# Keys' second rotary projection replaced by four ScalarE copies of 32-row blocks, from the fourth pair on

## The chip, the cores and the metric

The kernel runs on one core of a Trainium2 chip. The metric is the device time of the program in microseconds (us), taken as the median of several runs. Engines are named as in the profile: PE is TensorE's matmuls, PEld its weight loads, DVE is VectorE, ACT is ScalarE, POOL is GpSimd, SP is SyncE, which issues the DMAs.

## The reference

One decoder layer with three residual parts, each followed by a layer norm, on x of 32 sequences of 64 rows and 256 features:

```
x = layernorm(x + self_attention(x))            # 16 heads of 16, causal
x = layernorm(x + cross_attention(x, ctx))      # 8 heads of 8, rotary embedding
x = layernorm(x + ffn(x))                       # two quantised products, 256 -> 1024 -> 256
```

In the cross attention the second axis (64) holds the channels and the third (256) the positions. The part that the change touches is the rotary embedding of the keys:

```
k = Wk @ c + bk                                  # 64 x 256
half = k.shape[-1] // 2                          # of the 8 channels of a head
rot = concatenate([-k[half:], k[:half]])         # within each head
k = k * cos(pos) + rot * sin(pos)
```

`rot` is k with the two halves of each head's channels exchanged, and one half negated.

## The kernel before

**Tiling.** The 32 sequences are worked on as 16 pairs (`NPAIR`), each a tile of 128 partitions (two sequences of 64) and 256 columns. A first phase does both attentions of all pairs, and a second one the ffn.

**The first phase** is a software pipeline. `body(i)` is written once for each engine, runs for i = -1 to 15, and has 16 steps s. The body of i does the cross attention's maxima (`max_tile`, L971 on DVE) and exponentials (`exp_tile`, L780 on ACT) of pair i, some work of `prev = i - 1`, `nxt = i + 1`, `j = i + 2`, and the self attention and key projection of `a = i + 3`. In what follows a turn is one such body, and a step is one s. In each step PE does two products for a maximum (L581) and two for an exponential (L609), and in most also a group for something else. The instructions of each engine stand in its queue in the order in which they are written and are done in that order; engines meet in semaphores (`wait`).

**Maxima.** The products of a step land in one of two banks `mx_b`; `max_ready` lets PE write a bank when DVE has reduced the tile of two steps before. The exponentials have two banks `e_b` and `exp_ready` in the same manner.

**The general banks.** Three banks `g_b0`, `g_b1`, `g_b2` of 128 x 512 float32 serve all else. PE's helper `use` (L474) makes every use of a bank wait until the readers of the use before are done:

```
def use(bank, ev, pair, step):
    if bank.name in last_read:
        pe.wait_ge(*last_read[bank.name])
    last_read[bank.name] = (ev.sem, ev.at(pair, step))
```

**The rotary embedding.** `rotary_proj` multiplies the input with two weight matrices: "A", the projection, and "B", the same with its rows exchanged so that it gives the exchanged channels (`swap`). A goes to columns 0 to 255 of the bank, B to 256 to 511 (L558, L559; each float32 matmul is two records in the profile). The rows of both are laid out in the order of `by_parity` and `split`, so that the exchange is one of blocks of 32 partitions: 0 with 1, and 2 with 3. `rotate` on DVE then does two steps (L962): m = 0 is (A + bias) * cos, m = 1 is (B + bias) * sin, each with one count on `ro_sb`. Each is 128 x 256. `split_parts` on POOL adds the two and splits the sum into three bfloat16 parts (L906 to L916), which SP stores and loads again in expanded form (`KA`).

For the keys of a pair with number over 2 (`fresh`), that is pairs 3 to 15 in turns i = 0 to 12, PE does `rotary_proj("k", g_b[2], a)` in step 9, and DVE `rotate("k", g_b[2], a)` in step 10. The earlier three pairs' keys use other banks and are not touched.

**What stands around it.** In the order of the queues:

- PE: step 9 the key projection and `x_out_proj` of prev (L263); step 10 the transpose of the maxima (`max_transpose`, L595) and values (L626); step 11; step 12 `v_proj` (L495, from the pair after), `transpose_p(a)` (L523), values; step 13 `self_pv` (L536). `transpose_p` transposes the self attention's normalised probabilities `SP`, its first group into `g_b2` and its second into `g_b1`:

```
wait(pe, s_norm, a, 1)
for g in range(2):
    ps = use(g_b[2 - g], pt_sb, a, g + 1)
```

- DVE: step 4 the row maxima of the self scores (L924) after PE's `scores` (L510), and a subtraction (L932); step 7 another; step 9 `max_tile`, then `self_sum` (L941, L943); step 10 `max_tile`, `mt_low` (MR, L977), `rotate`, `norm2_stats` of prev (Y, L296, L299, L301); step 11 `max_tile`.
- POOL: `self_norm` (L898) after `self_sum`, `rstd` for prev (L314 to L318), `split_parts("k", a)`.
- ACT: step 9 the exponential and `mt_copy` (L774); steps 10 and 11 the exponentials; step 12 the exponential and `pt_copy` (L759), which copies the transposes. For some pairs a piece of the weights' preparation stands in step 11.

Of the kernel before, what the change touches and what calls it, by code (L numbers as in the profile page):

```python
# [21 lines left out]
ACT = mybir.ActivationFunctionType  # L22
# [5 lines left out]
P = 128  # L28
D = 256
# [51 lines left out]
def build_layer(nc, x, xT, ctx, wpT, woT, xW, xB, rows, w1T, w2T, attn_tables, rotary_tables, out):  # L81
    with ExitStack() as outer:
        es = outer

        def sb(name, shape, dt=F32):
            return es.enter_context(nc.sbuf_tensor(name, shape, dt))
# [4 lines left out]
        def sem(name):  # L91
            return es.enter_context(nc.semaphore(name))

        def event(name, steps=1):
            return Event(sem(name), steps)
# [12 lines left out]
        xw = {n: xw_all[:, k, :] for k, n in enumerate(XW)}  # L108
# [26 lines left out]
        g_b = [bank(f"g_b{n}") for n in range(2)]  # L135
# [26 lines left out]
        rot = {n: sb("rot_" + n, [P, 2, D]) for n in "qk"}  # L162
        full = {n: sb("full_" + n, [P, D]) for n in "qk"}
        part = {n: sb("part_" + n, [P, 3, D], BF16) for n in "qk"}
        QA = sb("QA", [P, 6, HH, D], BF16)
        KA = sb("KA", [P, 6, HH, D], BF16)
        VA = sb("VA", [P, 2, 2, 2, XH, 32])
# [33 lines left out]
        ro_ps = {n: event(n + "_ps") for n in "qk"}  # L201
        ro_sb = {n: event(n + "_rot", 2) for n in "qk"}
        split = {n: event(n + "_split", 5) for n in "qk"}
        xv_ps, xv_sb = event("xv_ps"), event("xv_sb")
        expand = {n: [sem(f"expand_{n}{p}") for p in range(3)] for n in "qk"}
        stored = {n: [sem(f"stored_{n}{p}") for p in range(2)] for n in "qk"}
        parts_hbm = {n: [nc.dram_tensor(f"parts_{n}{p}", (4, P, D), BF16, kind="Internal").ap() for p in range(2)] for n in "qk"}
# [14 lines left out]
        def wait(eng, ev, pair, step):  # L222
            eng.wait_ge(ev.sem, ev.at(pair, step))
# [5 lines left out]
        def real(pair):  # L229
            return 0 <= pair.v < NPAIR  # L230

        def fresh(pair):

            return real(pair) and pair.v > 2
# [236 lines left out]
        def _(pe):  # L471
# [76 lines left out]
            def rotary_proj(n, bank, j):  # L548

                pe.wait_ge(ld_cross, NCROSS)  # L550
                if n == "q":
                    wait(pe, ln1, j, 7)
                    src = XALL[:, j.v, :]
                else:
                    pe.wait_ge(ld_c[j.slot], 16 * (j.laps + 1))
                    src = C[:, j.slot, :]
                ps = use(bank, ro_sb[n], j, 2)
                nc.tensor.matmul(ps[:, 0:D], xw[n + "A"], src, start=True, stop=True)  # L558
                nc.tensor.matmul(ps[:, D:2 * D], xw[n + "B"], src, start=True, stop=True).then_inc(ro_ps[n].sem, 1)  # L559

            def xv_proj(v):

# [164 lines left out]
        def _(act):  # L727
# [40 lines left out]
            def mt_copy(i, b, g):  # L768
                wait(act, mt_ps, i, b + 1)
                before = i.plus(b - 1)  # L770
                if b == 1 or has(i, 1):
                    act.wait_ge(mrow[before.ring][1 - b], NMROW * (before.rounds + 1))

                nc.scalar.activation(MR[0:16, :], g_b[g][0:16, 0:P], ACT.Copy, scale=-1.0).then_inc(mt_sb.sem, 1)  # L774
# [14 lines left out]
            def norm1(a):  # L789
                wait(act, ln1, a, 6)  # L790
                nc.scalar.activation(XALL[:, a.v, :], Y1[:], ACT.Identity, bias=rs1[:, 2:3], scale=rs1[:, 1:2]).then_inc(ln1.sem, 1)

            def xv_copy(v):
                wait(act, xv_ps, v, 1)
                if has(v, 2):
                    wait(act, pv, v.plus(-2), 8)
                act.wait_ge(s_ones, 2)
                nc.scalar.activation(VA[:, v.p].rearrange("p s b h c -> p (s b) h c")[:, :, :, 0:XC],
                                     g_b[1][:, 0:D].rearrange("p (q h c) -> p q h c", q=4, h=XH),
                                     ACT.Copy).then_inc(xv_sb.sem, 1)  # L800
# [40 lines left out]
            def body(i):  # L841
                prev, nxt, j, a = i.plus(-1), i.plus(1), i.plus(2), i.plus(3)
                for s in range(16):
                    if real(i):
                        exp_tile(i, s)
                    if s == int(i.v == NPAIR - 1) and real(prev):
                        u_copy(prev)
                    if s == 0 and real(j):
                        norm1(j)
                    if s == 0 and fresh(a):  # L850
                        qk_copy(a, g_b[2])
                    if s == 1 and real(i):
                        mt_copy(i, 1, 0)
                    if s == 5 and real(prev):
                        at_copy(act, prev, 2)
                    if s == 7 and real(nxt):
                        xv_copy(nxt)
                    if s == 7 and fresh(a):
                        self_exp(a, 1)
                        self_exp(a, 0)  # L860
                    if s == 9 and real(nxt):
                        mt_copy(nxt, 0, 0)
                    if s == 12 and real(a):
                        pt_copy(a)
                    if s == 13 and real(prev):
                        norm2(act, prev)
                    if s == 13 and real(a):
                        ao_copy(a)
                    if s == 15 and real(i.plus(4)):
                        v_copy(i.plus(4), g_b[0])  # L870
                    if s == 15 and real(prev):
                        square_sum(act, prev)
                    if s in (3, 11) and W_SUM <= i.v < W_SUM + 4:
                        weight_sum(2 * (i.v - W_SUM) + s // 8)
                    if s in (3, 11) and W_ROUND <= i.v < W_ROUND + 4:
                        weight_round(2 * (i.v - W_ROUND) + s // 8)
# [43 lines left out]
        def _(dve):  # L920
# [35 lines left out]
            def rotate(n, bank, j):  # L956

                wait(dve, ro_ps[n], j, 1)
                if has(j, 1):
                    wait(dve, split[n], j.plus(-1), 2)  # L960
                for m, tab in ((0, cos), (1, sin)):
                    nc.vector.scalar_tensor_tensor(out=rot[n][:, m, :], in0=bank[:, D * m:D * m + D],  # L962
                                                   scalar=xb[n + "AB"[m]], in1=tab[:],
                                                   op0=ALU.add, op1=ALU.mult).then_inc(ro_sb[n].sem, 1)

# [41 lines left out]
            def body(i):  # L1007
                prev, nxt, j, a = i.plus(-1), i.plus(1), i.plus(2), i.plus(3)
                for s in range(16):
                    ahead, n = tile_at(i, s + AHEAD)  # L1010
                    if real(ahead):
                        max_tile(ahead, n)
                    if s == 2 and real(i):
                        mt_low(i, 1, 0)
                    if s == (2 if i.v >= 0 else 5) and real(j):
                        rotate("q", g_b[1], j)
                    if s == 3 and real(prev):
                        u_norm(dve, prev, 2)
                    if s == 4 and fresh(a):
                        row_max(a, 1)  # L1020
                        row_max(a, 0)
                        minus_max(a, 1)
                    if s == 7 and fresh(a):
                        minus_max(a, 0)
                    if s == 9 and real(a):
                        self_sum(a)
                    if s == 9 and real(a) and not fresh(a):
                        rotate("k", e_b[1], a)
                    if s == 10 and real(nxt):
                        mt_low(nxt, 0, 0)  # L1030
                    if s == 10 and fresh(a):
                        rotate("k", g_b[2], a)
                    if s == 10 and real(prev):
                        norm2_stats(dve, prev, 1)
                    if s == 14 and real(prev):
                        norm2_max(dve, prev)
                    if s == 15 and real(a):
                        norm1_stats(a)
                    if s == 14 and i.v == W_TOTAL:
                        weight_scale()  # L1040
                    if s == 4 and i.v == NPAIR - 1:
                        mean_square(dve, 0)
                    if s == 11 and i.v == NPAIR - 1:
                        factors(dve, 0)
                    if s == 1 and W_ROUND <= i.v - 1 < W_ROUND + 4:
                        for step in range(2):
                            for piece in range(2):
                                weight_clip(2 * (i.v - 1 - W_ROUND) + piece, step)
# [27 lines left out]

            prologue()
            bodies(dve, body)


# [469 lines left out]
```

## Time and profile before

| | |
|---|---|
| median of 3 runs | 543.01 us (540.65, 543.01, 547.83) |
| the profiled execution | 539.41 us, of which the span from the first to the last instruction is 537.3 us |
| busy in the span | PE 428.1 us (80%), DVE 442.1 (82%), ACT 374.3 (70%), POOL 287.1 (53%) |
| mean granted TensorE clock | 0.873 of full speed |

The profile is one execution, and its times are in microseconds from the start of the span. A line such as L559 is that of the kernel before, printed above. The busy time of PE is that of its matmuls, which overlap one another; what one costs the queue is read from start to start. "Idle before" names the engine and line whose work ended the wait.

### The profile page before, as it was taken

Reading aid. Unit: us, or ns where it says so; the run is one execution under the profiler, and the core shown is the slowest. Engines: PE = TensorE matmul, PEld = TensorE weight load, DVE = VectorE, ACT = ScalarE, POOL = GpSimd, SP = SyncE. Lnnn points to the kernel's source line nnn. Section 1 sums busy time; section 2 is a strip of 40 time slices with the busy share of each in tenths; the row PEclk is TensorE's granted clock in tenths of the full one; section 3 lists DMA queues with packets and bytes.
Section 4 is the critical chain, followed back from the end, with each engine's and each line's share of the span. In section 5 each row is a group of like instructions: output and inputs, shape, how many; then the busy total and the mean of one; then the engine's idle time right before and its main releaser. Section 6 shows DMA issues by size and latency. Waiting matters only on the chain. (4 is left out here: it accounts for less than half of the span.)

```text
span 537.3 us, 11851 instructions
## 1 busy us (share of the span) xinstructions
PE 428.1 (80%) x4098; PEld 231.1 (43%) x4098; DVE 442.1 (82%) x948; ACT 374.3 (70%) x700; POOL 287.1 (53%) x390
## 2 busy tenths in 40 slices
PE   6567799999999999999999999998876602555553
PEld 5354445445454554545545555443332201333332
DVE  3755787989889889799998998988749959999993
ACT  2232266678687786777877867677778778999983
POOL 5841646475474655645557446450124547767653
PEclk9676799999999999999999999999998855555557
DMA  6125326442332322323223232221000000000001
GB/s 226 46 77 182 93 57 187 113 114 69 82 96 63 113 70 67 108 52 111 71 64 112 66 95 69 61 89 42 3 0 1 1 0 1 11 30 20 31 30 40
DMA packets 51674, 37.07 MB, mean 69 GB/s; under 512 B 21408, under 2 KB 47648, under 8 KB 51488
## 3 DMA queue, kind: packets, MB, share of 16 engines
q1 hardware_dynamic: 51328, 36.10, 22.9%
q8 instruction: 33, 0.54, 0.4%
q10 hardware_dynamic: 288, 0.23, 0.2%
q14 instruction: 25, 0.20, 0.1%
HBM read 24.52 MB, written 10.49 MB: 65 GB/s over the span
## 5 line engine op out<-in xcount | busy, mean ns | idle before, releaser
L971 DVE TENSOR_REDUCE MX<-mx_b 128x2 f32<-128x512 f32 x256 | 167.1, 679 | 26.5 <-PE mx_b L581 25.4
L780 ACT ACTIVATE PB<-e_b 128x512 f32<-128x512 f32 x256 | 148.1, 592 | 55.2 <-PE e_b L609 54.0
L581 PE MATMUL mx_b<-KA,QA 48*128 48x256 bf16 x512 | 97.6, 275 | 11.5 <-DVE MX L971 10.8
L609 PE MATMUL e_b<-QA,KA 50*128 50x256 bf16 x512 | 97.1, 274 | 1.0 <-DMA QA<-MR 0.7
L626 PE MATMUL u_b<-PB,VA 128*32 128x256 f32 x1024 | 84.0, 391 | 2.0 <-ACT PB L780 1.5
L898 POOL TENSOR_TENSOR SP<-SP,srec 128x1024 f32<-128x1024 f32 x15 | 28.5, 1901 | 79.1 <-DVE srec L943 79.1
L581 PEld LDWEIGHTS mx_b<-KA,QA 48*128 48x128 bf16 x512 | 29.6, 94 | 86.7 <-issue 47.1
L1301 PE MATMUL r_b<-identh,Q 128*128 128x128 f16 x128 | 16.2, 305 | 39.5 <-ACT Q L1214 39.5
L1246 POOL TENSOR_TENSOR H<-H,row_tab 128x1024 f32<-128x1024 f32 x15 | 35.4, 2363 | 21.4 <-ACT H L1204 17.9
L1307 PE MATMUL z_b<-w2q,Q2T 128*128 128x256 bf16 x128 | 28.5, 400 | 19.3 <-ACT Q2T L1225 19.3
L888 POOL TENSOR_TENSOR KM<-QK,att_tab 128x512 f32<-128x512 f32 x31 | 32.0, 1052 | 21.4 <-ACT QK L734 21.4
L486 PE MATMUL g_b<-XT,wp 128*128 128x128 f32 x256 | 34.5, 290 | 4.7 <-DMA wp<-in_wpT 4.7
L626 PEld LDWEIGHTS u_b<-PB,VA 128*32 128x32 f32 x1024 | 22.4, 108 | 30.8 <-ACT PB L780 16.6
L314 POOL TENSOR_TENSOR rs<-mv,epsc 128x1 f32<-128x1 f32 x32 | 6.1, 189 | 54.3 <-DVE mv L301 38.3
L486 PEld LDWEIGHTS g_b<-XT,wp 128*128 128x128 f32 x256 | 31.5, 200 | 7.9 <-DMA wp<-in_wpT 4.7
L1301 PEld LDWEIGHTS r_b<-identh,Q 128*128 128x128 f16 x128 | 12.2, 139 | 46.6 <-ACT Q L1214 46.5
L609 PEld LDWEIGHTS e_b<-QA,KA 50*128 50x128 bf16 x512 | 28.5, 94 | 7.4 <-ACT PB L780 3.2
L759 ACT ACTIVATE PT<-g_b 128x512 f32<-128x512 f32 x32 | 17.7, 595 | 19.2 <-PE g_b L523 18.9
L1307 PEld LDWEIGHTS z_b<-w2q,Q2T 128*128 128x128 bf16 x128 | 15.9, 135 | 28.8 <-ACT Q2T L1225 23.4
L924 DVE TENSOR_REDUCE smax<-g_b 128x8 f32<-128x512 f32 x32 | 20.6, 686 | 8.8 <-PE g_b L510 8.8
L523 PE MATMUL g_b<-att_tab,SP 128*128 128x128 f32 x128 | 18.8, 296 | 8.8 <-POOL SP L898 4.7
L1422 DVE BATCH_NORM_STATS2 sth<-H 128x6 f32<-128x512 f32 x32 | 20.4, 680 | 3.5 <-ACT H L1208 3.5
(172 smaller groups left out, 1017.0 us busy)
## 6 DMA issues: line engine op xcount, KB each, us to landing
KA<-parts_k SPq DMA_DIRECT2D x64, 96.0 KB
QA<-parts_q SPq DMA_DIRECT2D x64, 96.0 KB
parts_q<-part_q SPq DMA_DIRECT2D x32, 128.0 KB, 1.9
parts_k<-part_k SPq DMA_DIRECT2D x16, 192.0 KB, 2.1
C<-in_ctx SPq DMA_DIRECT2D x16, 128.0 KB, 3.1
X<-in_x SPq DMA_DIRECT2D x16, 128.0 KB, 2.9
out_y<-O SPq DMA_DIRECT2D x16, 128.0 KB, 1.7
XT<-in_xT SPq DMA_DIRECT2D x15, 128.0 KB, 2.2
```

The source lines that it names most:

```text
L486: last = nc.tensor.matmul(ps[:, P * c:P * c + P], wp[:, k, P * c:P * c + P], XT[:, a.p, k, :], start=k == 0, stop=k == 1)
L581: m = nc.tensor.matmul(mx_b[n % 2][:, D * k:D * k + D], QA[low:low + K_MAX, 2 * i.ring + b, h, P * u:P * u + P], KA[low:low + K_MAX, 2 * i ...
L609: m = nc.tensor.matmul(e_b[n % 2][:, D * k:D * k + D], KA[low:low + K_EXP, 2 * i.ring + b, h, P * sc:P * sc + P], QA[low:low + K_EXP, 2 * ...
L626: last = nc.tensor.matmul(u_b[32 * j:32 * j + 32, D * b:D * b + D], VA[:, i.p, sc, b].rearrange("p h c -> p (h c)")[:, own:own + 32], PB[: ...
L780: nc.scalar.activation(PB[:, n % 4].rearrange("p e t -> p (e t)"), e_b[n % 2][:, :], ACT.Exp, scale=XC ** -0.5).then_inc(e_sb.sem, 1)
L888: ops.tensor_tensor(KM[:, c], QK[:, 2 + c, :].unsqueeze(1).broadcast_to([P, 4, P]), kmask.unsqueeze(2).broadcast_to([P, 4, P]), ALU.mult). ...
L898: ops.tensor_tensor(SP[:], SP[:], srec[:].unsqueeze(2).broadcast_to([P, SH, SEQ]), ALU.mult).then_inc(s_norm.sem, 1)
L924: nc.vector.tensor_reduce(smax[:].rearrange("p (c r k) -> p c r k", c=2, r=2)[:, :, r], g_b[r][:, :].rearrange("p (c k s) -> p c k s", c=2 ...
L971: nc.vector.tensor_reduce(MX[:, b, e, 2 * q:2 * q + 2, u], mx_b[n % 2][:, :].rearrange("p (e s) -> p e s", e=2), AXL.X, ALU.max).then_inc( ...
L1246: nc.gpsimd.tensor_tensor(H[:, i.v, :], H[:, i.v, :], gam, ALU.mult).then_inc(zg.sem, 1)
L1301: m = nc.tensor.transpose(r_b[j.p][:, P * k:P * k + P], low_half(Q2[:, j.p, P * k:P * k + P]), identh[:])
L1307: m = nc.tensor.matmul(z_b[j.p][:, 0:D], Q2T[:, j.p, k, :], w2q[:, k, :], start=k == 0, stop=k == 7)
```

## The change

For the keys of the fresh pairs the second matmul ("B") is left out. `rotary_proj` counts its semaphore up after the first one. On ACT a new function, `exchange_k`, stands in step 10 behind the exponential. It waits for the projection and for the rotation of the pair before, and then copies, in four instructions, 32 rows x 256 columns each from the bank to a new SBUF tile `KS` (128 x 256, float32), each block to the place of its neighbour. On DVE the sine step reads `KS` in place of the second half of the bank, and both steps wait for all four copies. The call of `rotate` for these pairs moves from step 10 to step 11, where it stands behind `max_tile` of step 11; in step 10 `norm2_stats` follows `mt_low` directly. PE's `use` is unchanged: the bank is free when both steps of `rotate` are done. Queries and the first three pairs' keys keep both matmuls.

```diff
@@ -162,6 +162,7 @@
+        KS = sb("KS", [P, D])
@@ -202,6 +203,7 @@
+        k_swap = event("k_swap", 4)
@@ -555,8 +557,12 @@
                 ps = use(bank, ro_sb[n], j, 2)
-                nc.tensor.matmul(ps[:, 0:D], xw[n + "A"], src, start=True, stop=True)
-                nc.tensor.matmul(ps[:, D:2 * D], xw[n + "B"], src, start=True, stop=True).then_inc(ro_ps[n].sem, 1)
+                first = nc.tensor.matmul(ps[:, 0:D], xw[n + "A"], src, start=True, stop=True)
+                if n == "k" and fresh(j):
+
+                    first.then_inc(ro_ps[n].sem, 1)
+                else:
+                    nc.tensor.matmul(ps[:, D:2 * D], xw[n + "B"], src, start=True, stop=True).then_inc(ro_ps[n].sem, 1)
@@ -790,6 +796,13 @@
+            def exchange_k(j, bank):
+                wait(act, ro_ps["k"], j, 1)
+                wait(act, ro_sb["k"], j.plus(-1), 2)
+                for k in range(4):
+                    to, at = slice(32 * k, 32 * k + 32), slice(32 * (k ^ 1), 32 * (k ^ 1) + 32)
+                    nc.scalar.activation(KS[to, :], bank[at, 0:D], ACT.Copy).then_inc(k_swap.sem, 1)
@@ -860,6 +873,8 @@
+                    if s == 10 and fresh(a):
+                        exchange_k(a, g_b[2])
@@ -958,8 +973,12 @@
+                swapped = n == "k" and fresh(j)
+                if swapped:
+
+                    dve.wait_ge(k_swap.sem, 4 * (j.v - 2))
                 for m, tab in ((0, cos), (1, sin)):
-                    nc.vector.scalar_tensor_tensor(out=rot[n][:, m, :], in0=bank[:, D * m:D * m + D],
+                    nc.vector.scalar_tensor_tensor(out=rot[n][:, m, :], in0=KS[:] if swapped and m else bank[:, D * m:D * m + D],
@@ -1028,7 +1047,7 @@
-                    if s == 10 and fresh(a):
+                    if s == 11 and fresh(a):
                         rotate("k", g_b[2], a)
```

## Rows read from the trace of the kernel before

**Rows 1.** Page, granted TensorE clock in 40 slices of the span (9 is 90% or more).

```profile
PEclk9676799999999999999999999999998855555557
```

**Rows 2.** Stages: window us, then busy us (xinstructions) of PE, PEld, DVE, ACT, POOL, clock, DMA.

```profile
300.00:330.00 30.00, 29.61 (x336) 16.21 (x335) 27.98 (x57) 22.25 (x49) 17.92 (x27) 1.00 0.26 75
192.88:204.57 11.69, 11.69 (x138) 6.72 (x137) 9.17 (x21) 9.19 (x22) 8.34 (x15) 1.00 0.36 105
183.82:192.52 8.70, 8.31 (x81) 4.02 (x77) 8.60 (x16) 6.13 (x13) 3.07 (x4) 1.00 0.20 47
```

**Rows 3.** Order of time, PE, turn 5, steps 9 to 12: start, us, instruction.

```profile
188.54 0.70 PE L558 MATMUL g_b<-C,xw_all 128*128 128x256 f32 x2
189.08 0.59 PE L559 MATMUL g_b<-C,xw_all 128*128 128x256 f32 x2
189.51 0.38 PE L263 MATMUL g_b<-AT,xw_all 128*128 128x256 f32 x1
...
191.36 0.28 PE L581 MATMUL mx_b<-KA,QA 48*128 48x256 bf16 x1
191.59 0.28 PE L609 MATMUL e_b<-QA,KA 50*128 50x256 bf16 x1
...
191.91 1.13 PE L495 MATMUL g_b<-wp,XT 128*128 128x256 f32 x4
192.88 1.04 PE L523 MATMUL g_b<-att_tab,SP 128*128 128x128 f32 x8
```

**Rows 4.** Order of time, DVE, turn 5, from the scores to step 11.

```profile
183.82 1.29 DVE L924 TENSOR_REDUCE smax<-g_b 128x8 f32<-128x512 f32 x2 [0.17 <-PE g_b L510]
...
186.22 1.28 DVE L971 TENSOR_REDUCE MX<-mx_b 128x2 f32<-128x512 f32 x2
...
190.67 0.63 DVE L971 TENSOR_REDUCE MX<-mx_b 128x2 f32<-128x512 f32 x1
...
191.64 0.88 DVE L962 SCALAR_TENSOR_TENSOR rot_k<-g_b,xb_all,rot_tab 128x256 f32<-128x256 f32 x2
192.44 0.47 DVE L296 SCALAR_TENSOR_TENSOR Y<-g_b,xb_all,XALL 128x256 f32<-128x256 f32 x1
...
193.51 0.66 DVE L971 TENSOR_REDUCE MX<-mx_b 128x2 f32<-128x512 f32 x1
```

**Rows 5.** Order of time, POOL, turn 5: the normalisation, and the split of the keys.

```profile
190.83 1.90 POOL L898 TENSOR_TENSOR SP<-SP,srec 128x1024 f32<-128x1024 f32 x1 [5.47 <-DVE srec L943]
...
194.81 0.73 POOL L906 TENSOR_TENSOR full_k<-rot_k 128x256 f32<-128x256 f32 x1
```

**Rows 6.** Order of time, ACT, turn 5: exponentials of steps 10 and 11, copies of step 15.

```profile
190.97 1.21 ACT L780 ACTIVATE PB<-e_b 128x512 f32<-128x512 f32 x2
...
197.21 0.38 ACT L742 ACTIVATE VS<-g_b 128x256 f32<-128x256 f32 x1
197.47 0.56 ACT L745 ACTIVATE VM<-g_b 64x128 f32<-64x128 f32 x2
```

**Rows 7.** Groups by line and form, 60 to 390 us: busy us, mean ns, idle before.

```profile
L791 ACT ACTIVATE XALL<-Y,rs 128x256 f32<-128x256 f32 x14 | 8.4, 601 | 8.5 <-POOL rs L318 8.5
```

**Rows 8.** Order of time, turns 0 and 12: key rotation and first transposes.

```profile
81.14 0.88 DVE L962 SCALAR_TENSOR_TENSOR rot_k<-g_b,xb_all,rot_tab 128x256 f32<-128x256 f32 x2
...
82.29 0.33 PE L523 MATMUL g_b<-att_tab,SP 128*128 128x128 f32 x1
...
346.24 0.88 DVE L962 SCALAR_TENSOR_TENSOR rot_k<-g_b,xb_all,rot_tab 128x256 f32<-128x256 f32 x2
...
347.38 0.44 PE L523 MATMUL g_b<-att_tab,SP 128*128 128x128 f32 x2 [0.81 <-POOL SP L898]
```

**Rows 9.** Instructions of line L309: ns min/median/max, first and last start us.

```profile
L309 DVE TENSOR_REDUCE amax<-XALL x16: 407/409/419, 108.8 to 410.9; 128x1 f32<-128x256 f32 x16
```

**Rows 10.** Order of time, PE, turn 5: first maximum product of step 7.

```profile
186.36 0.28 PE L581 MATMUL mx_b<-KA,QA 48*128 48x256 bf16 x1 [0.36 <-DVE MX L971]
```

**Rows 11.** Order of time, PE, turn -1: the transposes of pair 2.

```profile
61.36 1.85 PE L523 MATMUL g_b<-att_tab,SP 128*128 128x128 f32 x8
```

## The prediction

> **What bounds the kernel now.** I read first the page's TensorE clock and the table of stages. In the loop over pairs (about 60 to 390 us) the granted clock is at its upper level [rows 1], and PE is busy 29.61 of 30 us, DVE 27.98, ACT 22.25, POOL 17.92 [rows 2]. Two engines are nearly full, so a share of busy time does not say what an edit is worth; I went on to the order of time of one turn, that of pair a = 8 (i = 5, 183.8 to 204.6 us).
>
> The reader is to see a loop of two pieces there. From the first transpose of the probabilities (192.88) to the score products of the next pair (204.57) PE is busy 11.69 of 11.69 us: it waits for nobody [rows 2, 3]. The scores release DVE (183.82, and the same 21.90 us later), and from there DVE is busy 8.60 of 8.70 us until the end of the key rotation (192.52) [rows 2, 4]. On that DVE stretch lies the sum of the softmax; POOL normalises behind its reciprocal until 190.83 + 1.90 = 192.73, and PE's transposes start at 192.88 [rows 3, 5]. So the turn is: PE from transposes to scores, DVE from scores to the sum, POOL, transposes. In the last fresh pair, where PE has no value projection to do before, the trace shows it openly: PE stands idle 0.81 us for POOL's SP in front of the transposes [rows 8]. From a release to a start I count 0.05 us, as from DVE's MX (190.67 + 0.63 = 191.30) to the matmul that reuses its bank (191.36) [rows 3, 4].
>
> **What the change removes.** The second key projection is two matmul records (L559). Their place on PE is from 189.08 to 189.51, 0.43 us, since matmuls overlap; the weight loads lie under others [rows 3]. 13 pairs: 5.6 us of PE's time. What of it reaches the end? L263 and the whole of step 10 behind it start 0.43 us earlier. Then three things catch it up. Step 12's first matmul (191.36) needs DVE's MX of step 10, done at 191.30, and DVE did not get earlier: it works without a gap behind the sum [rows 3, 4]. Step 12's second (191.59) waited for the exponential of step 10, which now ends 0.43 us earlier, so it goes with the first: 0.23 us gained [rows 3, 6]. The transposes wait for POOL's 192.73 + 0.05 = 192.78: 0.10 us gained of 0.43. The saving alone would be worth 13 x 0.10 = 1.3 us.
>
> **What it adds on ACT.** Four copies of 32 rows x 256 from PSUM. The nearest rows are the 128x256 copy of VS, 0.38 us, after which the next instruction starts 0.26 us later, and the two VM copies, 0.56 us for both [rows 6]. Below: 4 x 0.27 = 1.1 us; above: 4 x 0.60 = 2.4 us by the 128x256 normalisation from SBUF [rows 7]. I take 0.38 each, 1.5 us. They stand behind the exponential of step 10. That began at 190.97; with the max transpose 0.43 us earlier it begins at 190.54, and the copies run from about 191.05 to 192.6. Queued behind them on ACT are the exponentials of steps 11 and 12 and the copies of PT. Two exponentials take 1.21 us [rows 6], so they end at about 193.8. PE needs the one of step 11, half of that earlier, only for the values behind the transposes, which end at 192.88 + 1.04 = 193.92 before and later after the change [rows 3]. So ACT's 13 x 1.5 = 20 us cost nothing as long as DVE asks for KS after 192.6; below it does.
>
> **What it moves on DVE.** Before, DVE does MX of step 10, MR, both rotations (0.80 us from start to next start), Y, two statistics, MX of step 11 [rows 4]. After, the rotations stand behind MX of step 11. MR stays; Y moves to 191.64; MX follows Y by 193.51 - 192.44 = 1.07 us, so 192.71, its input having long been written by PE; the next start after an MX is 0.60 us later (two of 0.68 us each take 1.28 together), so the rotations start at 193.31 and end 0.88 us later, 194.19 [rows 4]. The copies are ready at 192.6, 0.7 us before.
> The sine step reads KS from SBUF instead of PSUM. The trace has no such instruction; its price lies between the 0.41 us of a 256-column reduction in SBUF and the 0.48 us of now [rows 9, 4]. I take 0.41: 0.07 us gained in each of 13.
>
> **Where the move meets the path.** PE's bank helper makes each use of a bank wait for the last reader of the use before. The key projection of step 9 writes g_b2, and the next use of g_b2 is the first group of the transposes at step 12; it waits for both rotations, the cosine step that reads the bank and the sine step that no longer does. Before, the rotations ended at 192.52, 0.26 us ahead of POOL's 192.78: hidden. After, they end at 194.19, and the transposes start at 194.24 instead of 192.88: 1.36 us late. Behind the transposes PE has its whole queue in order: values, step 13, self values, and so on to the scores, 11.69 us without a gap to take the delay up [rows 2]. DVE, ACT and POOL all wait for PE there. The turn becomes 21.90 + 1.36.
>
> **The sum.** Pairs 4 to 14 (11 turns like this one): 11 x 1.36 = 15.0. Pair 15: the rotations started at 346.24; 346.24 + 2.55 (as 1.07, 0.60 and 0.88 above) + 0.05 = 348.84 against 347.38, 1.46 [rows 8]. Pair 3 has no Y behind its rotations: MX at 81.14, rotations 81.74 to 82.62, transposes 82.67 against 82.29, 0.38 [rows 8]. Together 16.8, less 13 x 0.07 = 0.9 for the sine step: 15.9 us. The saved 0.43 us is already in it: it is spent in waiting for the bank. POOL's split of the keys starts behind the statistics' root as before, and by then the rotation is done (194.19 against 194.81 before): no loss there, and none for the store and the loads of KA behind it. The profiled execution took 539.4 us (span 537.3); it becomes 555.3. The median of the runs shown is 543.0, 3.6 above the profiled one; with it 543.0 + 15.9 = 558.9, 2.9% slower.
>
> **Rivals.**
> - The bank is not what the transposes wait for last: the rotations would have to end before 192.78, that is, DVE would have to have 1.4 us to spare between scores and rotations. Against it: 8.60 of 8.70 us busy [rows 2]. If it is so all the same, the gain is between 1.3 us (the catch-up above) and 5.6 us (all of 13 x 0.43): 541.7 to 537.4, not slower. The point from which it decides is POOL's end, 192.73. Chance 0.11. The Trainium skill says (Perfetto Trace Analysis, "Identifying the Most-Contended Engine") that one improves a kernel by lightening its most occupied engine, while it warns there that matmul occupancy is a poor measure; by that rule the removal on PE would give the 5.6 us.
> - The delay is partly taken up: PE waits once more in a turn, for MX of step 5. That wait would have to give back its whole 0.36 us [rows 10]. Against it: DVE's stretch there is itself released by PE. Then 12 x 0.36 = 4.3 less: 554.6. Chance 0.08.
> - ACT becomes late: the copies start at 191.05 and DVE asks at 193.31, so they decide from 0.57 us each. With 0.60 each DVE waits 0.14 us more; with twice the 0.38 us of VS, 0.76 each, they are ready at 194.09 and DVE waits 0.8 us more per turn: 13 x 0.8 = 10.4, 569.4. For it: different rows each time. Against it: VM's two copies, on different rows too, take 0.56 together [rows 6]. Chance 0.08.
> - PE's clock falls in the new pause of about 1.6 us a turn. At the lower level the eight transposes of pair 2 took 1.85 us instead of 1.04 [rows 11, 3]. Against it: the clock stays up in the loop [rows 1]. If some turns lost 1 us more of this kind: about 570. Chance 0.04.
>
> **The numbers.** The forecast has the remaining 0.69: 559 us. Its own range, with the sine step from 0.41 to 0.48 us, the turns from 1.2 to 1.5 us and the 7 us between the runs of before, is 553 to 565. To hold 8 in 10 it takes in the case of the partly taken-up delay at its lower end and some of the late ACT at its upper: 551 to 566. What is left out is the not slower case (0.11) and the far parts of the last two (0.08). A measurement here tells about 2% from no change, 11 us. Slower by over 2%: the forecast, nearly all of the partly taken-up delay and the last two, less a tail, 0.85. Within 2%: 0.13. Faster by over 2% would need more than all of PE's saving: 0.02.
>
> **What would show it.** In the profile after: L523 starts right behind the end of the second rotation, and the idle time before it is put down to DVE's rot_k in 13 turns, over 15 us in all; POOL's SP ends about 1.5 us before L523 starts; the turn is 23.2 us, not 21.9; PE's busy share falls from 99% to about 91% (21.6 - 0.4 us in 23.2) and DVE's from 93% to 88%; the four copies take 0.3 to 0.4 us and end before MX of step 11 does; step 12's matmuls start 0.2 us earlier behind step 9 than now. It is wrong if L523 still follows POOL, if the rotation is found waiting for the copies, or if the 1.36 us shows up as a shorter wait elsewhere in the turn.

## The result and the profile after

| | before | after |
|---|---|---|
| median us | 541.94 (4 runs, 540.65 to 547.83) | 563.51 (4 runs, 563.47 to 569.25) |
| profiled execution us (span) | 539.41 (537.3) | 563.47 (561.6) |
| mean granted clock | 0.873 | 0.860 |

The changed kernel takes 1.042 times as long (95% interval 1.036 to 1.048). It is 21.6 us slower by the medians and 24.1 us by the two profiled executions; the forecast was 15.9 us more, 559 us. The kernel before has one run more here than in the table above, so its median differs. A second set of 6 runs beside others gave 566.2 against 543.7 us, 1.046 (1.041 to 1.051).

The lines have moved in the changed kernel: L525 are the transposes (L523 before), L981 the rotation (L962), L990 MX (L971), L913 POOL's normalisation (L898), L804 the copies.

The waits of PE over the whole span, changed kernel (engine, line waited for: us in total, times, longest us):

```profile
PE g_b L525 <- DVE rot_k L981: 19.3, 13, 2.6
```

The kernel before had no such wait. Now the transposes wait for the rotation in all 13 turns with a fresh pair. In order of time, turn 8, changed kernel (start, us, instruction, idle before and who ended it):

```profile
269.41 0.63 DVE L990 TENSOR_REDUCE MX<-mx_b 128x2 f32<-128x512 f32 x1
...
270.38 0.48 DVE L298 SCALAR_TENSOR_TENSOR Y<-g_b,xb_all,XALL 128x256 f32<-128x256 f32 x1
...
271.46 0.66 DVE L990 TENSOR_REDUCE MX<-mx_b 128x2 f32<-128x512 f32 x1
272.03 0.48 DVE L981 SCALAR_TENSOR_TENSOR rot_k<-g_b,xb_all,rot_tab 128x256 f32<-128x256 f32 x1
272.42 0.48 DVE L981 SCALAR_TENSOR_TENSOR rot_k<-KS,xb_all,rot_tab 128x256 f32<-128x256 f32 x1
```

```profile
269.57 1.90 POOL L913 TENSOR_TENSOR SP<-SP,srec 128x1024 f32<-128x1024 f32 x1 [5.47 <-DVE srec L958]
```

```profile
269.87 1.57 ACT L804 ACTIVATE KS<-g_b 32x256 f32<-32x256 f32 x4
271.46 0.60 ACT L786 ACTIVATE PB<-e_b 128x512 f32<-128x512 f32 x1
```

```profile
270.09 0.28 PE L587 MATMUL mx_b<-KA,QA 48*128 48x256 bf16 x1 [0.28 <-DVE MX L990]
...
270.49 1.10 PE L497 MATMUL g_b<-wp,XT 128*128 128x256 f32 x4
273.05 0.63 PE L525 MATMUL g_b<-att_tab,SP 128*128 128x128 f32 x4 [1.45 <-DVE rot_k L981]
```

These answer to [rows 3 to 6]. The probabilities are ready at 269.57 + 1.90 = 271.47 and PE's projection is through, but the bank is not free: the sine step ends at 272.90, and the transposes start at 273.05. PE stands still for 1.45 us. The copies were done at 271.44, 0.59 us before the rotation asked for them. The window of one turn and the stage that stood in [rows 2], changed kernel (window, its length, then busy us (xinstructions) of PE, PEld, DVE, ACT, POOL, clock, DMA):

```profile
267.30:290.60 23.30, 21.18 (x234) 11.07 (x232) 20.32 (x42) 18.29 (x41) 12.96 (x19) 1.00 0.28 78
300.00:330.00 30.00, 27.88 (x290) 15.07 (x286) 26.20 (x57) 23.83 (x54) 15.41 (x25) 1.00 0.31 91
```

PE is busy 27.88 of 30 us where it was 29.61. In the window of the turn PE's share is 91% and DVE's 87%; the prediction had 91% and 88%.

Read from the start of the first transpose to that of the next turn, a turn takes 23.37 us where it took 21.90. Some turns take 24.8 us, and there the transposes themselves are slow:

```profile
343.15 1.94 PE L525 MATMUL g_b<-att_tab,SP 128*128 128x128 f32 x8 [1.45 <-DVE rot_k L981]
```

That is near the 1.85 us of pair 2's transposes [rows 11], where the granted clock was 0.55; at 1.00 they took 1.04 [rows 3]. In a window over these slow transposes the granted clock is 0.50, the lower of its two levels (1.2 GHz of 2.4):

```profile
343.10:345.10 2.00, 1.95 (x12) 1.66 (x16) 0.50 (x1) 0.60 (x1) 1.92 (x4) 0.50 0.38 119
```

This is so in turns 3, 6, 11 and 12 of the profiled execution. The clock line of the page, which was at nine tenths or more through the loop [rows 1], shows only the later falls, since one of its slices is 14 us long:

```profile
PEclk9677799999999999999999998979799975555557
```

### The profile page after: what moved, and what is told of

Its sections match the earlier page's. It is cut to its first block and busy times, and to the rows that moved or that the text cites. A ratio compares the mean times of both kernels' runs of the same rounds, so it can differ in the third digit from the quotient of the medians.

```text
span 561.6 us, 11862 instructions
## 1 busy us (share of the span) xinstructions
PE 430.8 (77%) x4070; PEld 227.7 (41%) x4072; DVE 441.5 (79%) x948; ACT 393.8 (70%) x752; POOL 289.9 (52%) x390
## 5 line engine op out<-in xcount | busy, mean ns | idle before, releaser
L990 DVE TENSOR_REDUCE MX<-mx_b 128x2 f32<-128x512 f32 x256 | 167.9, 679 | 52.7 <-PE mx_b L587 52.4
L587 PE MATMUL mx_b<-KA,QA 48*128 48x256 bf16 x512 | 100.2, 284 | 14.8 <-DVE MX L990 14.8
L615 PE MATMUL e_b<-QA,KA 50*128 50x256 bf16 x512 | 99.1, 280 | 0.3
L632 PE MATMUL u_b<-PB,VA 128*32 128x256 f32 x1024 | 87.2, 407 | 2.1 <-ACT PB L786 1.6
L913 POOL TENSOR_TENSOR SP<-SP,srec 128x1024 f32<-128x1024 f32 x15 | 28.5, 1901 | 78.8 <-DVE srec L958 78.8
L525 PE MATMUL g_b<-att_tab,SP 128*128 128x128 f32 x128 | 22.5, 333 | 27.4 <-DVE rot_k L981 19.3
L525 PEld LDWEIGHTS g_b<-att_tab,SP 128*128 128x128 f32 x128 | 18.2, 173 | 32.7 <-issue 27.4
L1326 PEld LDWEIGHTS z_b<-w2q,Q2T 128*128 128x128 bf16 x128 | 15.9, 135 | 28.8 <-ACT Q2T L1244 23.4
```

Of the source, the lines that this page charges most:

```text
L525: last = nc.tensor.transpose(ps[:, P * j:P * j + P], SP[:, h:h + 2, :].rearrange("p h s -> p (h s)"), ident)
L587: m = nc.tensor.matmul(mx_b[n % 2][:, D * k:D * k + D], QA[low:low + K_MAX, 2 * i.ring + b, h, P * u:P * u + P], KA[low:low + K_MAX, 2 * i ...
L615: m = nc.tensor.matmul(e_b[n % 2][:, D * k:D * k + D], KA[low:low + K_EXP, 2 * i.ring + b, h, P * sc:P * sc + P], QA[low:low + K_EXP, 2 * ...
L632: last = nc.tensor.matmul(u_b[32 * j:32 * j + 32, D * b:D * b + D], VA[:, i.p, sc, b].rearrange("p h c -> p (h c)")[:, own:own + 32], PB[: ...
L913: ops.tensor_tensor(SP[:], SP[:], srec[:].unsqueeze(2).broadcast_to([P, SH, SEQ]), ALU.mult).then_inc(s_norm.sem, 1)
L990: nc.vector.tensor_reduce(MX[:, b, e, 2 * q:2 * q + 2, u], mx_b[n % 2][:, :].rearrange("p (e s) -> p e s", e=2), AXL.X, ALU.max).then_inc( ...
```

## The experiments

All were timed beside the kernel before in 3 or 5 rounds, not all on the same chip. "Turn" is the time between the first transposes of two turns, read in each run's own order of time; from turn 3 on the turns of one kernel agree within 0.02 us, apart from those with lower clock and where it is said otherwise; the last, from turn 11 to 12, is 21.82 us before. Turn 7's length, counted from turn 6, holds one more wait in all kernels (the weights' total, 23.16 us before) and is left aside.

| kernel | rotation | bank free after | turn us | ratio to before (95%) |
|---|---|---|---|---|
| before | step 10 | sine | 21.90 | 1 |
| after | step 11 | sine | 23.37 | 1.042 (1.036 to 1.048) |
| after_again | step 11 | sine | 23.37 | 1.046 (1.041 to 1.051) |
| move_only | step 11 | sine | 23.37 | 1.040 (1.032 to 1.048) |
| drop_only | step 10 | sine | 21.88 | 0.995 (0.991 to 0.998) |
| copies_step10 | step 10 | sine | 22.91 | 1.022 (1.011 to 1.033) |
| release_cos | step 11 | cosine | 22.98 | 1.028 (1.019 to 1.037) |
| fill_pause | step 11 | sine | 23.37 | 1.039 (1.033 to 1.045) |
| swap_release | step 11 | cosine, groups exchanged | 22.48; 22.66 to 22.76 | 1.018 (1.013 to 1.023) |
| norm_first | step 10, behind Y | cosine, groups exchanged | 22.06; 22.66 to 22.76 | 1.012 (1.007 to 1.018) |
| norm_first_w5 | step 10, behind Y | cosine, groups exchanged | 22.06 | 1.002 (0.999 to 1.005) |
| idle_copies | step 10 | sine | 22.51; 23.33 to 23.43 | 1.027 (1.022 to 1.032) |

Where two lengths stand, the second is that of the turns in which ScalarE has a piece of the weights in step 11 (2 to 5 and 7 to 10), and the first that of turn 11.

**Which part of the change costs: the move alone.**

```diff
--- before
-                    if s == 10 and fresh(a):
+                    if s == 11 and fresh(a):
                         rotate("k", g_b[2], a)
```

> The kernel before with one edit: the keys' rotation of pairs 3 to 15 stands in step 11 on DVE; both matmuls stay, there are no copies. Theory (the bank wait): everything lost comes from this move. DVE ends the rotation as late as in the changed kernel, so the transposes start as late behind DVE's MX of step 10, the turn is 23.3 to 23.4 us instead of 21.9, and the time is 18 to 24 us over the kernel before, the same as the changed kernel within 4 us. Rival A (ScalarE: the 1.6 us of copies a turn cost the time): no loss, within 2 us of before. Rival B (the missing matmul makes the pause in which PE's clock falls): about 17 us over before, with transposes at the upper clock in every turn.

Measured: 565.2 us against 545.0, and the turn is 23.37 us, to the hundredth that of the changed kernel. Turn 8 in order of time, DVE and under it PE:

```profile
275.30 0.66 DVE L971 TENSOR_REDUCE MX<-mx_b 128x2 f32<-128x512 f32 x1
275.88 0.87 DVE L962 SCALAR_TENSOR_TENSOR rot_k<-g_b,xb_all,rot_tab 128x256 f32<-128x256 f32 x2
...
276.89 0.30 PE L523 MATMUL g_b<-att_tab,SP 128*128 128x128 f32 x1 [1.27 <-DVE rot_k L962]
```

The removed matmuls, the copies and KS account for nothing of the longer turn. PE's pause is 1.27 us here and 1.45 in the changed kernel, and there PE also stands 0.28 us in front of step 12's first product, which it does not here: these 0.18 and 0.28 us are where the saving of the second matmul (0.43 us) ends up.

Rival B, that the clock falls only where the matmul is missing, is neither shown nor excluded. It expected about 17 us over before; the interval of the ratio is 17 to 26 us. As it said, no transposes of turns 2 to 12 were slow in this execution, but there was a stretch at the lower clock in turn 1 (102 to 108 us, 0.50), and others behind the last fresh pair. The part that the clock has is taken up below.

**What the removal is worth.**

```diff
--- before
-                nc.tensor.matmul(ps[:, D:2 * D], xw[n + "B"], src, start=True, stop=True).then_inc(ro_ps[n].sem, 1)
+                if n == "k" and fresh(j):
+                    first.then_inc(ro_ps[n].sem, 1)
+                else:
+                    nc.tensor.matmul(ps[:, D:2 * D], xw[n + "B"], src, start=True, stop=True).then_inc(ro_ps[n].sem, 1)
...
-                    ... in0=bank[:, D * m:D * m + D],
+                    ... in0=bank[:, 0:D] if n == "k" and fresh(j) else bank[:, D * m:D * m + D],
```

> The kernel before without the second key matmul of pairs 3 to 15; the sine step reads the first matmul's columns instead, so the exchanged channels are left out and the output is not the reference's. No copies, no move. Theory: of the 0.43 us of PE's time a turn only 0.1 us reaches the end, since the transposes wait for POOL's normalisation: 1 to 2 us faster than before in all (ratio 0.996 to 0.999), turn 21.8 us. Rival (PE is the bound): 5.6 us faster, ratio 0.990, turn 21.47 us.

Measured: 542.2 us against 545.0. The turn is 21.88 us, 0.02 less than before, where PE being the bound would have given 21.47. Turn 8:

```profile
260.87 1.90 POOL L901 TENSOR_TENSOR SP<-SP,srec 128x1024 f32<-128x1024 f32 x1 [5.46 <-DVE srec L946]
...
261.40 0.28 PE L584 MATMUL mx_b<-KA,QA 48*128 48x256 bf16 x1 [0.28 <-DVE MX L974]
...
262.83 0.33 PE L523 MATMUL g_b<-att_tab,SP 128*128 128x128 f32 x1
```

Most of the 0.43 us goes at step 12's first product: PE stands there 0.28 us for MX of step 10. POOL ends at 262.77 and the transposes start 0.06 us later; before, they started 0.15 us behind POOL. So they stand 0.09 us earlier, and the values behind them start 1.02 us after their start instead of 0.96, which takes most of that back. The measured ratio, 0.995, says 0.2 to 0.9% (1 to 5 us); the turns explain 0.3 us of it. Where the rest would come from is open: the runs of before reach from 539.8 to 546.7 us, and the traced execution of drop_only (548.9 us, the longest of its ten) can't show it.

**What makes the rotation late doesn't matter.**

```diff
--- after
-                    if s == 11 and fresh(a):
+                    if s == 10 and fresh(a):
                         rotate("k", g_b[2], a)
```

> The changed kernel with the keys' rotation back in step 10. DVE then waits for the copies, which end 2.03 us behind the start of MX of step 10 in the changed kernel, where it could have begun at 0.97. Theory (the bank wait sets the turn by the end of the rotation, whatever makes it late): rotation starts at 2.1, ends at 3.0, transposes at 3.1 against 2.2 before and 3.6 in the changed kernel: turn 22.8 us, 10 to 14 us over before, 8 to 12 us under the changed kernel. Rival (position in DVE's queue is what costs, not the time of its end): turn 21.9 us, no loss.

Measured: turn 22.91 us, 556.7 against 545.0 us. Turn 8:

```profile
268.63 0.48 DVE L981 SCALAR_TENSOR_TENSOR rot_k<-g_b,xb_all,rot_tab 128x256 f32<-128x256 f32 x1 [1.22 <-ACT KS L804]
269.03 0.48 DVE L981 SCALAR_TENSOR_TENSOR rot_k<-KS,xb_all,rot_tab 128x256 f32<-128x256 f32 x1
...
269.65 0.41 PE L525 MATMUL g_b<-att_tab,SP 128*128 128x128 f32 x2 [1.00 <-DVE rot_k L981]
```

DVE now stands 1.22 us for the copies, with Y and MX queued behind, and still the turn is 0.46 us shorter than with the move, as much as the rotation's end is earlier: 3.04 us behind the start of MX of step 10 in place of 3.49. The end of the rotation sets the turn.

**The wait itself.** PE counts the bank as free after the cosine step:

```diff
--- after
-                ps = use(bank, ro_sb[n], j, 2)
+                ps = use(bank, ro_sb[n], j, 1 if n == "k" and fresh(j) else 2)
```

> The changed kernel, but PE counts the bank g_b2 as free after the cosine step of the key rotation, the last that reads it, not after the sine step. Theory (the transposes wait for that count): they start 0.39 us earlier, the turn is 22.97 us instead of 23.37, 5 us less in 13 turns, and more if fewer turns fall to the lower clock: 5 to 10 us under the changed kernel. Rival (the wait is for POOL or for ScalarE): no change.

Measured: 559.7 us against 545.0; turn 22.98 us, 0.39 us less, which is the sine step from start to start. Turn 8:

```profile
269.56 0.48 DVE L981 SCALAR_TENSOR_TENSOR rot_k<-g_b,xb_all,rot_tab 128x256 f32<-128x256 f32 x1
269.95 0.48 DVE L981 SCALAR_TENSOR_TENSOR rot_k<-KS,xb_all,rot_tab 128x256 f32<-128x256 f32 x1
...
270.18 0.30 PE L525 MATMUL g_b<-att_tab,SP 128*128 128x128 f32 x1 [1.06 <-DVE rot_k L981]
```

PE starts at 270.18 while the sine step still runs until 270.43: it no longer waits for it. So the wait is the bank's, and not one for the data.

**The changed kernel once more**, for the spread.

> The changed kernel itself, beside the kernels below on one chip: turn 23.37 us, 20 to 24 us over before. Its spread from run to run shows how many turns fall to the lower TensorE clock.

Measured: 566.2 us (564.2 to 569.0), turn 23.37; transposes of turns 1, 3, 6, 11 and 12 at the lower clock in its profiled execution.

**The clock.** PE gets work in the pause, whose results nobody reads:

```diff
--- after
                         v_proj(i.plus(4), g_b[0])
+                    if s == 12 and real(i.plus(4)) and fresh(a):
+                        for rep in range(3):
+                            nc.tensor.matmul(g_b[0][:, D:2 * D], xw["kB"], C[:, a.slot, :], start=True, stop=True)
```

> The changed kernel with three more key matmuls (six records, 1.3 us) on PE in the pause of 1.5 us between the value projection and the transposes of turns 0 to 11; nothing reads their results. Theory (about 5 us of the loss is TensorE's clock falling in the pause): the turn stays 23.37 us, no transposes run at 1.9 us, and the time is 3 to 7 us under the changed kernel. Rival (the clock falls by chance, not by the pause, or the whole loss is in the turn's length): same as the changed kernel within 1.5 us. Rival (PE's work costs even in the pause): slower by some of 12 x 1.3 = 16 us.

Measured: 562.5 us, on the same chip 3.7 us under the changed kernel, with ratios of 1.039 (1.033 to 1.045) and 1.046 (1.041 to 1.051), whose intervals overlap a little. Turn 8:

```profile
271.34 1.10 PE L497 MATMUL g_b<-wp,XT 128*128 128x256 f32 x4
272.27 1.46 PE L692 MATMUL g_b<-C,xw_all 128*128 128x256 f32 x6
273.89 0.30 PE L525 MATMUL g_b<-att_tab,SP 128*128 128x128 f32 x1 [0.16 <-DVE rot_k L984]
```

The pause of turns 1 to 11 is 0.16 us in place of 1.45, the turn is the same 23.37 us, and none of the transposes of turns 0 to 12 ran at the lower clock: each took 1.04 to 1.07 us. 12 x 1.3 = 16 us of extra matmuls cost nothing. So PE's time at this place is worth nothing in the changed kernel. The 4 us that the kernel is faster fit the theory that a fall of the clock follows some of the pauses; beside the spread I call the direction likely and the size not settled. Two things don't fit it in full: turn 12's pause of 2.56 us is not filled in this kernel, and its transposes took 1.06 us all the same; and the clock still falls behind the last fresh pair, as in the changed kernel (390 to 400 us: 0.52).

**Away from the bank.** The two groups of transposes are exchanged on top of the earlier release, so that the first goes to a bank that is free:

```diff
--- release_cos
-                    ps = use(g_b[2 - g], pt_sb, a, g + 1)
+                    ps = use(g_b[1 + g], pt_sb, a, g + 1)
```

(and the same exchange in ScalarE's copy of the transposes, `pt_copy`).

> The changed kernel with the bank counted free after the cosine step, and the two groups of transposes exchanged: the first goes to g_b1, which is free, the second to g_b2. Theory (only the bank waits): the first group starts right behind POOL's normalisation, 1.1 us earlier than with the release alone, but the second still waits for the cosine step, so only its own 0.48 us is gained: turn 22.5 us, 12 x 0.6 = 7 us over before and some for the clock: 6 to 12 us over before. Rival (the wait is for something else that ends with the rotation, as the DVE queue): turn 22.98 us.

Measured: 550.9 against 543.7 us. In turns without a weight piece 22.48 us, as expected; 22.66 to 22.76 in the others, which was not. Turn 8, where the second group still waits for the rotation, and PE once more for ScalarE's copies of the transposes:

```profile
266.62 0.66 PE L525 MATMUL g_b<-att_tab,SP 128*128 128x128 f32 x4 [0.39 <-DVE rot_k L981]
...
268.37 0.69 PE L538 MATMUL g_b<-PT,VM 128*32 128x64 f32 x32 [0.20 <-ACT PT L765]
```

**The rotation in the shadow of the copies.** In step 10, behind the statistics of the second norm:

```diff
--- swap_release
                     if s == 10 and real(prev):
                         norm2_stats(dve, prev, 1)
-                    if s == 11 and fresh(a):
+                    if s == 10 and fresh(a):
                         rotate("k", g_b[2], a)
```

> On top of the exchanged groups and the earlier release, the key rotation stands in step 10, behind the second norm's statistics and ahead of MX of step 11: the statistics fill the time in which the copies run. Theory: the cosine step begins at 2.1 us behind MX of step 10 and ends at 2.6, just as the second group of transposes is due, so the turn is 21.9 to 22.1 us and the time that of before within 1% (ratio 0.995 to 1.008): the removal and the copies are worth nothing, and the loss of the change was all in where the rotation stood. Rival (ScalarE's copies or the exchange itself cost): turn at least 0.4 us longer than before, 5 us or more over before.

Measured: 548.3 against 543.7 us, ratio 1.012, over the expected 1.008 at most. Turn 11 took 22.06 us, as expected, but the turns with a weight piece 22.66 to 22.76. What they wait for, turn 4:

```profile
172.50 1.57 ACT L804 ACTIVATE KS<-g_b 32x256 f32<-32x256 f32 x4
174.10 0.60 ACT L786 ACTIVATE PB<-e_b 128x512 f32<-128x512 f32 x1
174.59 0.62 ACT L818 ACTIVATE w2q<-w2f 128x512 bf16<-128x512 f32 x1
...
175.68 1.08 ACT L765 ACTIVATE PT<-g_b 128x512 f32<-128x512 f32 x2
...
176.86 0.69 PE L538 MATMUL g_b<-PT,VM 128*32 128x64 f32 x32 [0.57 <-ACT PT L765]
```

PT's copies stand in ACT's queue behind the copies of KS, two exponentials and the weight piece, and PE waits 0.57 us for them. The theory on the bank holds, but it was not all: with the bank's wait gone, ScalarE is late.

**ScalarE's part, taken away.** The weight pieces of step 11 go to step 5:

```diff
--- norm_first
-                    if s in (3, 11) and W_SUM <= i.v < W_SUM + 4:
-                        weight_sum(2 * (i.v - W_SUM) + s // 8)
+                    if s in (3, 5) and W_SUM <= i.v < W_SUM + 4:
+                        weight_sum(2 * (i.v - W_SUM) + s // 5)
```

(and the same for `weight_round`).

> The kernel with the rotation behind the second norm's statistics, the groups exchanged and the early release, and with the weight pieces that ScalarE does in step 11 of turns 2 to 5 and 7 to 10 moved to step 5. In that kernel without the last edit the turns with a weight piece took 22.66 to 22.76 us and turn 11, without one, 22.06: PE waited 0.6 us for the copies PT behind the weight piece. Theory (ScalarE is late only where copies and weight piece come together): all turns take 22.06 us, the time is 4 to 6 us under that kernel and within 0.6% of before. Rival (the 0.6 us come from the copies alone): turns stay at 22.7 us.

Measured: 545.5 against 544.6 us, 1.002 (0.999 to 1.005), and 22.06 us in all turns from 3 on. This kernel computes the same with the second matmul left out and the copies in, and it stands within half a per cent of the kernel before. It doesn't beat it: 0.16 us a turn is left. In turn 8 the copies end at 260.47, the cosine step runs from 260.61 to 261.09, and the second group of transposes starts at 261.14; the values start 1.17 us behind the first transpose instead of 0.96. The kernel before with the weight pieces moved in the same way was not run.

**ScalarE's part, by itself.** The kernel before with four copies more in step 10:

```diff
--- before
+            def idle_copies(j):
+                act.wait_ge(ld_cross, NCROSS)
+                for k in range(4):
+                    to, at = slice(32 * k, 32 * k + 32), slice(32 * (k ^ 1), 32 * (k ^ 1) + 32)
+                    nc.scalar.activation(KS[to, :], cos[at, :], ACT.Copy)
...
+                    if s == 10 and fresh(a):
+                        idle_copies(a)
```

> The kernel before with four ScalarE copies of 32 rows x 256 a turn in step 10 of turns 0 to 12, from a constant table in SBUF to a tile that nobody reads; both matmuls stay and nothing is moved. It measures ScalarE's part alone. Theory (the copies are free only under the wait for the bank): the copies end at about 2.4 us behind MX of step 10, the exponentials of 11 and 12 and the weight pieces follow, and PT's copies come 0.4 us late in turns without a weight piece and 1.2 us late in the eight with one: 8 to 12 us over before, turns of 22.2 to 22.4 and 23.0 to 23.2 us. Rival (my prediction's sentence that ScalarE's 20 us cost nothing by themselves): no loss, turn 21.9 us.

Measured: 557.0 against 544.6 us, 12.5 us more, turns of 22.51 us and of 23.33 to 23.43 us: all somewhat over what was expected. Turn 8:

```profile
267.76 1.69 ACT L798 ACTIVATE KS<-rot_tab 32x256 f32<-32x256 f32 x4
269.46 0.60 ACT L781 ACTIVATE PB<-e_b 128x512 f32<-128x512 f32 x1
270.09 0.81 ACT L819 ACTIVATE w1f<-w1f,rnd,winv 128x512 f32<-128x512 f32 x1
...
271.28 1.07 ACT L760 ACTIVATE PT<-g_b 128x512 f32<-128x512 f32 x2
...
272.46 0.69 PE L537 MATMUL g_b<-PT,VM 128*32 128x64 f32 x32 [1.38 <-ACT PT L760]
```

So the copies, which cost almost nothing in the changed kernel, cost 0.7 to 1.5 us a turn where the bank's wait is not there to cover them. The two losses lie beside each other and don't add up: each alone makes a turn of up to 23.4 us, and both together make one of 23.37. (From SBUF a copy took 0.41 us, from PSUM 0.375, so this run has 0.12 us too much a turn; the rest of what it is over the expectation is not explained.)

## Why the prediction was right

**The sign and the mechanism held at each step.** The transposes wait for the bank g_b2, whose last reader is the key rotation; the move sets that reader behind Y and MX of step 11. From MX of step 10 to the start of the rotation the prediction had 193.31 - 190.67 = 2.64 us, and the trace has 272.03 - 269.41 = 2.62. Step 12's first product waits for MX of step 10 (0.28 us idle in front of it, 0.05 us behind MX's end), as reckoned, and the rest of step 12 starts 0.2 us earlier behind step 9 than before. The saving of 0.43 us is found again as idle time: 0.28 us there, and 0.18 of a longer pause in front of the transposes (1.45 against 1.27 us). The delay is not taken up anywhere: from the transposes to the next scores PE needs 11.72 us, before 11.69.

**The sizes.** The turn grew by 1.47 us instead of 1.36 - 0.07 = 1.29. Two terms of a turn were mis-sized. The sine step from SBUF was put at 0.41 us after a reduction [rows 9]; it takes the same as from PSUM:

```profile
L804 ACT ACTIVATE KS<-g_b x52: 372/375/377, 79.2 to 366.0; 32x256 f32<-32x256 f32 x52
L981 DVE SCALAR_TENSOR_TENSOR rot_k<-KS,xb_all,rot_tab x13: 474/477/478, 81.3 to 367.3; 128x256 f32<-128x256 f32 x13
```

(instructions of tile KS, changed kernel: ns min/median/max.) And the time from the end of the rotation to the start of the transposes is 0.15 us, not the 0.05 seen behind MX and POOL. Over 11 turns these are 2.0 us.

**The clock.** It was a rival with a chance of 0.04, as something instead of the forecast; it came on top of it. The two profiled executions stand 24.3 us apart in span. By the starts of transposes and of the ffn's first quantisation (QB, at 398.04 and 424.25 us) this is: 0.4 us less up to turn 0; 0.4 more in turn 1; 11 x 1.46 = 16.1 more in the lengths of turns 2 to 12; 4.4 more because the transposes of turns 3, 6 and 11 ran at the lower clock; 5.6 more between the last fresh pair's transposes and the ffn, where the lower clock stood in two stretches (388 to 408 us: 0.74, before 0.99); 1.9 less in the ffn. So the mechanism of the forecast gives 16.5 us, and about 8 us lie in stretches in which the clock was another in this execution. fill_pause is some 4 us faster, as much as the slow transposes cost. It does not mend the stretch behind the last fresh pair: from those transposes to the ffn's first QB its profiled execution took 56.2 us, the changed kernel's 56.3, and before 50.7. Why the clock falls in some turns and not in others with the same pause is open.

**What was luck.** The measured 563.5 us lie in the range of 551 to 566, but near its upper end, and the range reached so far for a late ScalarE, which did not come. The clock, for which the sum had nothing, filled that room. With the mechanism alone the time would have been near 559 us; in the second set, at 566.2 us, even the range was used up.

**The cover of the copies.** "So ACT's 13 x 1.5 = 20 us cost nothing as long as DVE asks for KS after 192.6" was right in its result and too narrow in its reason. The copies took 1.57 us and were ready 0.59 us before they were asked for. But the prediction looked only at the exponential of step 11, and not at PT's copies, which stand behind them on ACT and which PE needs in step 13. They came in time only because the transposes that they copy were late: ACT itself waits for these in turn 8.

```profile
273.71 1.09 ACT L765 ACTIVATE PT<-g_b 128x512 f32<-128x512 f32 x2 [0.47 <-PE g_b L525]
```

The copies are seen once in front of the rotation: in turn 0, where no Y stands before it, DVE waits 0.28 us for them. The prediction's term for pair 3 had left that out.

```profile
80.88 0.48 DVE L981 SCALAR_TENSOR_TENSOR rot_k<-g_b,xb_all,rot_tab 128x256 f32<-128x256 f32 x1 [0.28 <-ACT KS L804]
```

idle_copies shows the price without that cover, 12.5 us. The rival "not slower", in which the bank is not the last, had overlooked this too: by what idle_copies and norm_first show, it would not have come out as no loss.

**The not slower case** needed 1.4 us to spare on DVE and did not come; drop_only gives 0.02 us a turn where the prediction had 0.10: the transposes had started 0.15 us behind POOL's end and now start 0.06 behind it, but the values behind them start 0.06 us later after them than before. The rule that the prediction cited from the Trainium skill (Perfetto Trace Analysis, "Identifying the Most-Contended Engine"), to lighten the most occupied engine, would have given 5.6 us; the turn shows 0.3 us in 13 turns. The same section of the Trainium skill says that the busy share of matmuls is not a good measure of how close a kernel is to its roofline; no run here measures that distance, but a share of 29.61 in 30 us did not mean that time saved on PE would show.

## What to carry to other kernels

When an instruction that reads a PSUM bank is moved back in its queue, look up who writes that bank next: the move costs that writer all of the delay that it had no room for, whatever the engines' busy shares. Here the rotation ended 1.64 us later behind MX of step 10, and the transposes started 1.43 us later. A matmul saved on the fullest engine is worth only what lies between it and the next wait on another engine, here 0.02 of 0.43 us; and work put on a less busy engine has to be followed to everything queued behind it there, since another stall may be what hides it, and the loss comes out when that stall is mended.

## What the hardware showed that was not expected

- PE's clock fell behind some pauses of 1.45 us (in turn 12, 2.56 us) in a loop in which PE is else busy: transposes of 1.69 to 1.94 us in place of 1.06 in 4 and 5 of 13 turns of two executions of the changed kernel, and turns 3, 6, 11 and 12 in both. With the pause filled to 0.16 us none were slow. The pause is not the whole condition: in move_only (1.27 us, in turn 12 2.33) and in fill_pause's turn 12 (2.56 us) no transposes were slow either, while those of turn 12 were in release_cos (2.17 us, 1.94) and in copies_step10 (2.11 us, 1.50).
- Four copies of 32 rows x 256 columns to other rows take 0.375 us each and 0.40 from start to start, as long as a copy of 128 rows x 256 columns (0.38).
- A two-operand step of 128x256 float32 on DVE took 0.477 us with its first operand from SBUF, and 0.480 with it from PSUM (the rotation before).
